# Five fp32 weight products in rounded and low parts, both batches side by side, in a fused three-layer kernel

## The reference, cut to what matters

```
def self_attn(x, Wq, Wk, Wv):
    Q, K, V = (x @ Wq, x @ Wk, x @ Wv)
    energy = jnp.einsum('bqd,bkd->bqk', Q, K)
    lengths = jnp.sum(energy[:, 0] != 0, axis=-1)
    energy = jnp.where(pad | causal, NEG_INF, energy)
    score = jax.nn.softmax(energy / np.sqrt(DK), axis=-1)
    return jnp.einsum('bqk,bkd->bqd', score, V)
z = self_attn(x, Wq1, Wk1, Wv1)
x = layer_norm(x + z, ln1_g, ln1_b)
z = cross_attn(x, context, Wq2, Wk2, Wv2)
x = layer_norm(x + z, ln2_g, ln2_b)
```

## Time and profile before

| | us |
|---|---|
| median of 3 runs | 267.46 (267.41 to 269.32) |
| the profiled execution | 268.02 |
| its span, first to last instruction | 266.3 |
| PE busy | 236.0 (89%) |
| DVE, POOL, ACT busy | 169.7, 97.9, 87.3 |
| mean granted TensorE clock | 0.955 of full |

### The profile page before, as it was taken

How to read it: one execution, slowest core, us unless ns; L and a number is a source line. 1 busy time by engine, 2 the same in 40 slices (tenths; PEclk the granted TensorE clock), 3 DMA queues, 4 the chain that set the end, 5 groups by cost and what they waited for, 6 DMA issues and landing times.

```text
span 266.3 us, 3035 instructions
## 1 busy us (share of the span) xinstructions
PE 236.0 (89%) x1153; PEld 164.1 (62%) x1153; DVE 169.7 (64%) x301; ACT 87.3 (33%) x144; POOL 97.9 (37%) x80
## 2 busy tenths in 40 slices
PE   6899959899999988999889999991688769999895
PEld 6869648789778767686544444440344238899761
DVE  2216963378559976621827276779766686979781
ACT  2105420273197568121014545420110311240210
POOL 6002620179049765430402007587413422442000
PEclk9999989999999999999997999995699968999999
DMA  7999994001799994029600897000000000000002
GB/s 267 385 417 452 412 416 178 1 0 28 284 423 429 416 426 204 2 81 427 279 0 2 241 428 318 0 0 0 0 0 2 0 0 0 2 0 1 2 0 79
DMA packets 6350, 43.98 MB, mean 165 GB/s; under 512 B 832, under 2 KB 832, under 8 KB 1472
## 3 DMA queue, kind: packets, MB, share of 16 engines
q1 hardware_dynamic: 6336, 43.80, 40.7%
HBM read 43.27 MB, written 0.52 MB: 164 GB/s over the span
## 4 chain that ended last, share of the span: by engine, by line
PE 68%; DVE 17%; ACT 6%; POOL 4%; issue 2%; DMA 1%; DVEq 0%; POOLq 0%; ACTq 0%
PE psum L381 63%; ACT slots L1333 5%; PE psum L385 4%; POOL small L1575 2%; DVE ring_r L820 2%; DVE small L796 1%; DVE slots L978 1%; DMA slots<-xin 1%; DVE slots L998 1%; DVE slots L814 1%; POOL slots L1584 1%; DVE small L913 1%; ACT ring_r L1333 1%; DVE slots L1265 1%; POOL small L1641 1%
## 5 line engine op out<-in xcount | busy, mean ns | idle before, releaser
L381 PE MATMUL psum<-ring,slots 128*128 128x512 f32 (+3 forms) x228 | 95.6, 572 | 4.2 <-ACT slots L1333 4.1
L381 PEld LDWEIGHTS psum<-ring,slots 128*128 128x128 f32 (+1 forms) x228 | 41.7, 200 | 48.6 <-issue 41.5
L1333 ACT ACTIVATE slots<-psum 128x512 f32<-128x512 f32 (+3 forms) x51 | 27.6, 552 | 118.2 <-PE psum L381 72.6
L1580 POOL TENSOR_TENSOR ring_r<-ring,ring_r 128x640 fp32r<-128x640 f32 x16 | 41.5, 2605 | 44.0 <-ACT ring_r L1333 44.0
L381 PE MATMUL psum<-slots,ring 128*128 128x128 f32 x448 | 54.4, 282 | 2.5 <-ACT slots L1333 2.1
L381 PEld LDWEIGHTS psum<-slots,ring 128*128 128x128 f32 x448 | 53.3, 198 | 5.1 <-ACT slots L1333 2.9
L381 PE MATMUL psum<-ring_r,slots_r 128*128 128x512 f32 x192 | 46.5, 397 | 1.1 <-ACT slots_r L1333 0.7
L381 PEld LDWEIGHTS psum<-ring_r,slots_r 128*128 128x128 f32 x192 | 35.3, 188 | 10.0 <-issue 2.2
L1575 POOL TENSOR_TENSOR small<-small,mhalf 128x1 f32<-128x1 f32 x16 | 14.9, 931 | 59.5 <-DVE small L800 59.4
L1333 ACT ACTIVATE ring_r<-ring 128x2048 fp32r<-128x2048 f32 (+1 forms) x17 | 31.7, 1866 | 13.7 <-PE psum L381 12.8
L820 DVE TENSOR_TENSOR ring_r<-ring,ring_r 128x1408 fp32r<-128x1408 f32 x16 | 29.3, 1837 | 5.0 <-ACT ring_r L1333 5.0
(11 more groups left out here) (148 smaller groups left out, 207.8 us busy)
## 6 DMA issues: line engine op xcount, KB each, us to landing
ring<-blocks SPq DMA_DIRECT2D x36, 1024.0 KB, 11.0
bc<-vecs SPq DMA_DIRECT2D x1, 3072.0 KB, 28.3
bc<-vecs SPq DMA_DIRECT2D x1, 1280.0 KB, 6.6
slots<-xin SPq DMA_DIRECT2D x2, 256.0 KB, 3.9
bc<-vecs SPq DMA_DIRECT2D x1, 512.0 KB, 10.3
y<-slots SPq DMA_DIRECT2D x2, 256.0 KB, 2.0
colv<-cols SPq DMA_DIRECT2D x1, 14.0 KB, 8.9
```

Source lines behind the costliest of these rows:

```text
L381: return t.matmul(o_, l, r, start=first, stop=last)
L1333: return a.activation(o, x, func, **kw)
L1580: g.tensor_tensor(ring_r[:, p, CUT:], ring[:, p, CUT:], ring_r[:, high(name), CUT:], ALU.subtract).then_inc(*split_lowg.inc(name))
```

## The change

The five weights q1, k1, v1, q2, k2 join the list SPLITS, so ACT, DVE and POOL split them too. A new function `both` multiplies q1, k1, q2, k2: it holds a 128 x 128 piece of the weight and streams both batches' 256 turned columns in fp32r, 48 matmuls for a weight: high x high (first the weight's row groups 0 and 1, then 2 and 3), high x low of x, low x high. The products lie in two banks, each with one half of the output features for both batches, and are read out by halves, not by batches. The turned x, x1 and q2 are kept as high parts (ACT, or DVE for x of batch 1) and low parts (`rows_low`, `q2_split`, DVE). v1 goes through `three`. q1's split is made in two halves of its own. In `three` the waits for the low parts are moved behind the first four matmuls, and those for the low part of x (or of the softmax weights) to the last four.

x of batch 1 is fetched ahead of q1. Both self-attentions now run side by side: on PE every step is done for batch 0 and then for batch 1, both x1 are turned, and q2, k2 follow for both at once; then scores(0, 0 to 3), scores(1, 0), count2(0), scores(1, 1), shut_out(0), scores(1, 2), turn_p(0, 0 and 1), scores(1, 3), turn_p(0, 2 and 3). The orders of DVE, ACT and POOL follow. The diff, cut to its core:

```diff
-SPLITS = [f"ct{b}{n}" ...] + [f"c{b}{n}" ...]
+SPLITS = ["q1", "k1", "v1", "q2", "k2"] + [f"ct{b}{n}" ...] + [f"c{b}{n}" ...]
             eng.dma_start(X[0], xin[0, :, :]).then_inc(s_x[0], 16)
+            eng.dma_start(X[1], xin[1, :, :]).then_inc(s_x[1], 16)
             fetch("q1")
-            eng.dma_start(X[1], xin[1, :, :]).then_inc(s_x[1], 16)
+            def three(o_, xs, lows, name, first, last):
+                ws = parts(name)
                 s.wait_ge(*split_high.at(name))
+                for c in range(4):
+                    mm(o_, xs[0](c), ws[0][:, c, :], first and c == 0, False)
                 s.wait_ge(*split_low.at(name))
                 s.wait_ge(*split_lowg.at(name))
+                for c in range(4):
+                    mm(o_, xs[0](c), ws[1][:, c, :], False, False)
+                for low_at in lows:
+                    s.wait_ge(*low_at)
+                for c in range(4):
+                    i = mm(o_, xs[1](c), ws[0][:, c, :], False, last and c == 3)
+                return i
+            def both(name, hi, lo, bk):
+                wh, wl = parts(name)
+                s.wait_ge(*split_high.at("q1a" if name == "q1" else name))
+                for pair in range(2):
+                    if pair == 1:
+                        s.wait_ge(*split_high.at(name))
+                        if name == "k2":
+                            s.wait_ge(*evict[1].at("q2"))
+                    for e in range(4):
+                        for c in (2 * pair, 2 * pair + 1):
+                            both_mm(wh, hi, e, c, bk, c == 0 and e % 2 == 0, False)
+                for b in range(2):
+                    s.wait_ge(*(q2_low[b].at("q2") if name == "k2" else x_low[b].at("x1" if name == "q2" else "x")))
+                for e in range(4):
+                    for c in range(4):
+                        both_mm(wh, lo, e, c, bk, False, False)
+                s.wait_ge(*split_low.at(name))
+                s.wait_ge(*split_lowg.at(name))
+                for e in range(4):
+                    for c in range(4):
+                        i = both_mm(wl, hi, e, c, bk, False, e % 2 == 1 and c == 3)
+                    if e % 2:
+                        i.then_inc(*prod[e // 2].inc(name))
+            def both_mm(w, x, e, c, bk, first, last):
+                return mm(psum[:, bk + e // 2, (e % 2) * 256:(e % 2 + 1) * 256], w[:, c, e * 128:(e + 1) * 128],
+                          x[:, c, :], first, last)
             turned_rows(0, "x", Y[0], 0)
-            q1(0)
-            k1(0)
+            turned_rows(1, "x", Y[1], 4)
+            q1()
+            k1()
             v1(0)
             e1(0)
...
             e1(1)
             v1(1)
+            count1(0)
             count1(1)
...
+            em(0)
+            em(1)
+            pv1(0)
+            pv1(1)
             turned_rows(0, "x1", Z[0], 0)
...
             turned_rows(1, "x1", Z[1], 4)
...
+            q2()
+            k2()
+            for n in range(4):
+                scores(0, n)
+            scores(1, 0)
             count2(0)
+            scores(1, 1)
             shut_out(0)
...
 # DVE
+            norm(0, "x", Y[0], X[0])
+            norm(1, "x", Y[1], X[1])
+            v.tensor_copy(bcols(T8_r, 1), quarters(4)).then_inc(*turned_v.inc("x"))
+            rows_low(0, "x")
+            rows_low(1, "x")
+            low("q1")
+            low("k1")
+            low("v1")
...
+            pT(0)
             pT(1)
+            low("k2")
+            add1(0)
             add1(1)
+            norm1(0)
             norm1(1)
+            rows_low(0, "x1")
+            rows_low(1, "x1")
+            low("ct00")
+            q2_split(0)
+            q2_split(1)
+            low("ct01")
             k2_split(0)
+            k2_split(1)
+            low("ct02")
...
 # ACT
+            copy_turned(0, "x", T8_r, 0)
+            split("q1")
+            split("k1")
+            split("v1")
+            half_out(0, "q1", T10, 1)
+            half_out(1, "q1", T10, 2)
+            split("q2")
+            out(0, "v1", Vs[0], bank(0))
+            split("k2")
             exp1(0)
+            exp1(1)
+            out(1, "v1", Vs[1], bank(4))
             split("ct00")
...
 # POOL
+            low("q1")
+            low("k1")
+            low("v1")
+            low("q2")
+            low("k2")
             deviation(0, "x1")
             deviation(1, "x1")
-            for name in SPLITS[3:]:
+            for name in SPLITS[5:]:
                 low(name)
```

More of the change, by code:

```diff
@@ L26 @@
 NTH = {n: [m for m in BLOCKS if PLACE[m] == PLACE[n]].index(n) + 1 for n in BLOCKS}
-SPLITS = [f"ct{b}{n}" for b in range(2) for n in range(4)] + [f"c{b}{n}" for b in range(2) for n in range(4)]
+SPLITS = ["q1", "k1", "v1", "q2", "k2"] + [f"ct{b}{n}" for b in range(2) for n in range(4)] + [f"c{b}{n}" for b in range(2) for n in range(4)]
 CUT = 1408
@@ L286, in is_turned @@
         def is_turned(b, name):
-            return turned_v.at("x1") if b and name == "x" else turned[b].at(name)
+            return turned_v.at("x") if b and name == "x" else turned[b].at(name)
         def loaded(name):
@@ L425, in count, with q1 @@
+            def both_mm(w, x, e, c, bk, first, last):
+                return mm(psum[:, bk + e // 2, (e % 2) * 256:(e % 2 + 1) * 256], w[:, c, e * 128:(e + 1) * 128],
+                          x[:, c, :], first, last)
             def count(b, o_, src, name):
                 mm(o_, ones[0:1, :], src, True, True).then_inc(*prod[b].inc(name))
[L430 to L436, removed]
+            def q1():
+                for b in range(2):
+                    s.wait_ge(*is_turned(b, "x"))
+                both("q1", T8_r, T6_r, 1)
@@ L438, in v1, with k1 @@
+            def k1():
+                both("k1", T8_r, T6_r, 5)
             def v1(b):
-                s.wait_ge(*evict[b].at("q1"))
-                natural(b, "v1", bcols(T8, b), 4 * b + 1, "v1")
+                xs = [lambda c, of=of: of[:, c, b * 128:(b + 1) * 128] for of in (T8_r, T6_r)]
+                three(bank(4 * b), xs, [], "v1", True, True).then_inc(*prod[b].inc("v1"))
             def e1(b):
-                s.wait_ge(*evict[b].at("q1"))
-                s.wait_ge(*k1_in[b].at("k1"))
+                for h in range(2):
+                    s.wait_ge(*evict[h].at("q1"))
+                    s.wait_ge(*k1_in[h].at("k1"))
@@ L464, in pv1, with q2, k2 @@
                     *prod[b].inc("pv"))
[L468 to L474, removed]
+            def q2():
+                for b in range(2):
+                    s.wait_ge(*turned[b].at("x1"))
+                both("q2", T8_r, T6_r, 1)
+            def k2():
+                s.wait_ge(*evict[0].at("q2"))
+                both("k2", T10_r, T16_r, 5)
             def scores(b, n):
                 name = f"ct{b}{n}"
-                s.wait_ge(*evict[b].at("k2"))
-                s.wait_ge(*k2_low[b].at("k2"))
+                for h in range(2):
+                    s.wait_ge(*evict[h].at("k2"))
                 xs = [lambda c, of=of: of[:, c, b * 128:(b + 1) * 128] for of in (T12_r, T6_r)]
-                three(bank(4 * b + n), xs, name, True, True).then_inc(*score[b].inc(str(n)))
+                three(bank(4 * b + n), xs, [k2_low[h].at("k2") for h in range(2)], name, True, True).then_inc(
+                    *score[b].inc(str(n)))
             def count2(b):
@@ L1475, in _ @@
             split("ct12")
-            out(1, "q2", bcols(T10, 1), quarters(5))
-            out(1, "k2", bcols(T12_r, 1), quarters(6))
+            split("ct13")
             exp2(0, 0)
             exp2(0, 1)
-            split("ct13")
             p_out(0, 0)
```

150 lines of the change are left out of this document (66 added, 84 removed), and 2 rows, old and new, of the table prod.

## The result

| | before | changed |
|---|---|---|
| median, 4 runs each | 268.15 us | 277.33 us |
| ratio, changed to before | | 1.035 (1.031 to 1.039) |
| profiled execution | 268.02 | 278.43 |
| its span | 266.3 | 276.7 |
| mean granted clock | 0.955 | 0.924 |

The kernel before has one run more here than ahead of the prediction, so its median is 268.15 and not 267.46. An execution more than 1.5% above the fastest of its kernel is left out of the ratios (one of 4 in experiment 1, the traced one, two of 11 in 7, four of 12 in 10, one of 29 of the kernel before beside 9 to 12).

The account below looks back on a forecast made before the run. The prediction took PE, busy 89% of the span, to bound the kernel. +3.2 up to turn_p(1, 0) and -0.9 for later waits gave +2.3 on the median of 267.46: 269.8 us, range 267.0 to 272.5.

Parts of the forecast that it names:

- Start: Before q1: x's fetch ahead of q1's, then normalization, turning, copy, split; q1 starts at 9.25, not 7.84, 1.4 us on the path.
- I take 1.8 again: At q2, after PE's long idle time: the clock falls and costs 1.8 us, as q2(0) lost before.
- Sum: Whole kernel: +3.2 up to turn_p(1, 0), -0.9 after it, +2.3 us in all; 269.8 us, range 267.0 to 272.5.
- The pace of `both`: q1, k1, q2, k2: 0.12 us a matmul, 5.8 us a weight (5.1 to 6.0), -6.0 us for four weights.
- The rival of dear products: Products of `both` aren't cheaper: 0.21 us a matmul, +17 us, 287 us in all; chance 0.05.
- The trough: Between v1(1) and q2: PE idle some 11 of 15.2 us, q2 from 43.7; it eats what PE saves.
- The softmax of batch 0: From scores to gathers: PE waits 1.65 us before turn_p(0, 0) at 80.85; later gather waits delay turn_p(1, 0) to 101.5.
- the wait that I forecast inside gather(0, 0): gather(0, 0) asks for POOL's low part of c00 at 86.3, ready at 88.0: a wait of 1.7 us.
- `three` with later waits: After turn_p(1, 0): gather(1, 0)'s first four matmuls need only p_out, 0.9 us earlier; -0.9 us.
- the clock stays down longer: Slower rival: 1.2 GHz from the trough's first pause to q2's end, 4.9 us more, 274.7 us; chance 0.16.

Follow-up runs that it names:

- experiment 1: Changed kernel with the fetch of batch 1's x behind q1's again; ratio 1.038 to the kernel before.
- experiment 7: Kernel before with only the changed kernel's later waits in `three`; ratio 0.993 to the kernel before.
- Experiment 10: Changed kernel, but q2 and k2 in full fp32 by batch, k2_split(0) before low(ct01), kh's scaling moved, products of ones at start and batch 0's pause; ratio 0.992.
- 9: Changed kernel with products of ones in every pause, POOL's ct00 low part held back, maxima(0) moved ahead, kh's scaling moved back; ratio 1.005 to the kernel before.
- 12: Changed kernel with q1's fetch ahead of both x; ratio 1.040 to the kernel before.
- experiment 11: Kernel before with both fetches of x ahead of q1's; ratio 1.007 to the kernel before.
- experiment 2: Changed kernel with 13 unread products of ones between turning x of batch 1 and q1; ratio 1.026 to the kernel before.
- Experiment 3: Changed kernel's side-by-side order with all five weights in full fp32, without their splits and low parts; ratio 1.054 to the kernel before.
- experiment 6: Changed kernel with unread products of ones in every PE pause of the first 85 us; ratio 1.008 to the kernel before.
- experiment 5: Changed kernel with k1's fetch and all behind it held until batch 1's x has landed; ratio 1.030 to the kernel before.
- 8: Kernel before with the later waits in `three` and products of ones, 9 before turning x1 of batch 0 and 3 behind; ratio 0.987.
- 4: Changed kernel, but q2 and k2 in full fp32 by batch, order of the kernel before from scores(0, 0) on; ratio 1.031 to the kernel before.

## Why the prediction was wrong

The sign was right and the size was not: +2.3 forecast, +9.2 by the medians, +10.4 in the profiled executions. Two steps failed. The first is in "Start", where I took q1's block to be there when ACT was free. The second is "I take 1.8 again": the clock was priced in one place, at q2, and it fell in four places, from 9.6, 37, 44 and 88 us. (The range under "Sum" doesn't follow from its own terms either: they give 265.5 to 272.1.) Step by step, with the delay that each adds to my times:

| milestone | mine | measured | added |
|---|---|---|---|
| q1's first product | 9.25 | 11.21 | +2.0 |
| v1(1) ends | 28.5 | 32.5 | +2.0 |
| q2 starts | 43.7 | 49.0 | +1.3 |
| scores(0, 0) start | 57.8 | 63.7 | +0.6 |
| turn_p(0, 0) | 80.85 | 87.6 | +0.9 |
| gather(0, 0) | 85.4 | 93.7 | +1.5 |
| turn_p(1, 0) | 101.5 | 109.6 | -0.2 |

**Start, the landing: +2.0.** I had the chain x, normalization, turning, copy, split. It ran 0.6 us earlier than I wrote it, with ACT's copy done at 7.6 and not 8.2, since the four turns took 0.66 us and not the 1.09 of the kernel before. But the split then waited 2.43 us for a block whose landing I had not priced. The forecast held that x would land 0.7 us later and never asked the same of q1 behind it. Experiments 11 and 1 show the landing moving with the order, 12 that putting q1 first only makes x the late one.

**Start, the clock: +2.0.** That wait made a pause of 3.3 us, and the clock fell within it: 14.1 us for q1 and k1, 11.8 with products of ones (2). Experiment 2 changes nothing else; 1.4 us of its gain are there at the end of v1(1), the 2.3 less the overrun of 0.9.

**The pace of `both`: right.** One product took 283 ns in the trace, and 67 of them at full clock stand in this timeline of the changed kernel from 55 to 64 us:

```profile
54.76 8.18 PE L386 MATMUL psum<-slots_r,ring_r 128*128 128x256 f32 x67
```

(8.18 - 0.28) / 66 = 0.120 us, as taken; a weight is 5.75. The rule of the Trainium skill ("TensorE: Matmul & The Clock Gate", Part 3) that I set against it would have made it 10.2 by my estimate, and this trace disagrees. The rival of dear products falls with it. Experiment 3 says the same from the other side: without the parts the side-by-side order is 5 us slower still.

**The trough: 15.2 forecast, 16.5 measured.** The mechanism and nearly the size. When the clock was kept up (6) 15.5 remained, so about 1.0 of the 1.3 goes with the clock. norm1(1)'s centring, 2.02 us beside POOL's low part for 0.74, was not in my chain either; as 15.5 remained with it, other steps of the chain must have been about as much too long. Experiment 10 takes the trough apart by batch, with the clock up, and is 3.3 us less than side by side (9), even in full fp32; from q1's first product to turn_p(1, 0) the traces give 1.8. It changes the order behind the trough and the splits too, so what the trough alone costs stays open.

**The clock in q2: +0.6.** 1.8 taken; the clock stayed at 0.50 for 5 us after the start of q2, not 3.6.

**The softmax of batch 0: +0.9, then +1.5.** I had PE idle for 1.65 before turn_p(0, 0), and it was 2.09. I gave that pause no price beyond itself, and then scores(1, 3) took 4.29 us for the 2.8 of its twelve products: the clock again. Such a fall can't be counted on: in experiments 2 and 3 the same pause, 2.06 us, was followed by 3.02 us for these products, while in 1, 5 and 12 (2.05 to 2.09) the clock fell. The slow scores(1, 3) also paid for the wait that I forecast inside gather(0, 0): with scores(1, 3) slow, POOL's low part of c00 was nearly there in time, so the 1.7 us of that wait shrank; with the clock up (6) it is 1.36. count2(1) waited 1.28, where I had 1.3.

**`three` with later waits: right.** -0.9 forecast. From turn_p(1, 0) to the first product of gather(1, 0) are 2.95 us, 2.11 in experiment 7. The 1.9 us of its ratio are more than this edit explains; what its trace has besides is q1 0.28 earlier, a shorter fall of the clock in q2(0) (5.18 for 5.46), and no fall near 143 us.

**The rivals.** The slower one, "the clock stays down longer", had the right agent in one place only. Its 4.9 us were to come from the trough and q2; there it gave 1.0 + 0.6. The rest came after two waits, 3.27 us before q1 and 2.09 before turn_p(0, 0). The clock in all places, by experiment 6 against the changed kernel, is worth 7.2 us of the 9.2. With it up the change still costs 2.1 us (1.008), where my sum without its 1.8 of clock has 0.5. The queues are 0.9 of that difference by the ratios (9), 2.1 by the traces; the rest was not separated from the landing. And 1.008 flatters the change, for the kernel before has its own fall at 37 us. With the clock kept up in the first 100 us of both and the later waits in both, 6 stands at 1.008 and 8 at 0.987, run beside each other: side by side and in parts costs 5.6 us. This is the cost of the order, the late start and the supply of the gathers together, net of what the products save.

**Open.** Why the first block lands so late behind both small x. After its issue it took 4.8 to 5.0 us when it was first or had one x ahead (kernel before, 1, 12). With both ahead it took 6.8 (11), 7.1 (6), 7.7 (4), 8.1 (10), 8.2 to 8.3 (changed, 2, 3, 5), and at most 6.5 in 9. The order of the first fetches is the same in all of these (5 only holds k1 back), and each landing is read from one execution, so whether the kernel or the execution makes the difference isn't known. The estimate under experiment 5 fits blocks behind q1 moving before its last piece; why they do so with both x ahead and hardly otherwise isn't shown. Open too is why the clock fell after the pause before turn_p(0, 0) in the changed kernel and experiments 1, 5 and 12, and not in 2 and 3, and why it fell between 143 and 157 us in some executions only.

## What to carry to other kernels

Two chains that run beside each other hide each other's waits: before the products of two batches are put side by side, count what stands between them that only the other batch hid. Price every pause that the new order makes twice, once for itself and once for the clock after it, and ask of each transfer that is moved back when the one behind it will land. The part worth keeping was the small one: waits moved to where the operand is needed (0.993, of which the trace gives 0.8 us to the edit), with the clock kept up by products that nobody reads (0.987). And follow two traces to their ends before a difference is given to an edit: here 1.7 us of it lay some 25 us behind the last changed instruction.

## What I had not expected of the hardware

- The clock fell after pauses of some 2 to 3 us: after 3.3 us at the start (7.94 to 11.21, the window from 9 us at 0.82 already), and after 2.09 us before turn_p, where it fell at about 88.4, with PE at work again since 87.6. In experiment 2, after the same pause of 2.06 us (83.61 to 85.67), it stood at 1.00 from 80 to 92. In experiment 11 a wait of 1.74 us was enough, with a gap of 0.72 before it; in experiment 5 it stood at 1.00 through a pause of 2.81 us. So the length of the last pause alone doesn't decide.
- The granted clock doesn't show the whole pace. In experiments 2, 3, 4, 5, 9 and 10 it stands at 1.00 through the start, and still the first products run slower. In 5 q1 and k1 take 13.3 us, in 2 they take 11.8, and the first nine of them 2.26 us, where a pace of 0.12 gives 1.24. In 9 the 18 records of ones take 3.55 us for the 2.17 of 6.
- 13 products of ones (26 records, 4.14 us, experiment 2) in a wait kept the clock at 1.00 and cost 0.9 us where they ran over.
- An instruction of DVE with two SBUF inputs, 0.74 us for batch 0, took 2.02 us beside POOL's low part of 640 columns. "SBUF — State Buffer" of the Trainium skill has that lock ("Who interferes with whom"), and the trace agrees; with POOL held back (9) the same instruction took 0.75.
